# Two mixture-of-experts layers: gate and up computed transposed, each block's gate and up weights loaded into a ring of four pairs

## The reference

```python
# layer 0: E=16 experts, inner width 64, 2 experts for each token, besides a shared expert
hmid = silu(x @ w1[e].T) * (x @ w3[e].T) * combine
moe_out = hmid @ w2[e].T
# layer 1: E=32 experts, inner width 128, 4 experts for each token
gate = minimum(x @ w_gate[e] + b_gate[e], 7.0)
up = clip(x @ w_up[e] + b_up[e], -7.0, 7.0)
activated = (up + 1.0) * gate * sigmoid(1.702 * gate)
out = sum over the 4 of topk_weight * (activated @ w_down[e] + b_down[e])
```

## Time and profile before

| | us |
|---|---|
| median of 3 runs | 2014.76 (2012.57 to 2014.78) |
| the profiled execution, its own time | 2019.52 |
| its span, first to last instruction | 2017.7 |

### The profile page before, as it was taken

One profiled execution on the slowest core, in us unless ns is written; L12 is line 12 of the kernel. 1 busy time (PEld: TensorE's weight loads), 2 busy tenths in 40 slices (PEclk: granted clock), 3 DMA queues, 4 the chain that ended last, 5 costly groups with the idle time before them and its releaser, 6 DMA issues. The chain is left out here.

```text
span 2017.7 us, 47121 instructions
## 1 busy us (share of the span) xinstructions
PE 1637.8 (81%) x14340; PEld 1188.0 (59%) x14341; DVE 1447.6 (72%) x3040; ACT 950.5 (47%) x2964; POOL 1163.5 (58%) x1253
## 2 busy tenths in 40 slices
PE   4999999999999999799487429887884159999943
PEld 3777777777777777466366304444443148887822
DVE  3898998889989899666122267998996136666668
ACT  2888888878888788333133104333331023333300
POOL 1666666666666666356366404487885546666622
PEclk9999999999999999899689859998985579999965
DMA  5300000000000000212444240011115434444456
GB/s 174 118 16 16 16 16 16 16 16 16 16 18 21 16 16 8 84 65 81 143 140 126 96 148 22 12 64 58 66 56 211 166 104 146 143 150 131 124 197 220
DMA packets 100988, 164.76 MB, mean 82 GB/s; under 512 B 20031, under 2 KB 75884, under 8 KB 100336
## 3 DMA queue, kind: packets, MB, share of 16 engines
q1 hardware_dynamic: 75184, 104.37, 16.4%
q0 software_dynamic: 22272, 56.15, 7.6%
q10 hardware_dynamic: 3456, 3.34, 0.5%
HBM read 94.26 MB, written 75.76 MB: 84 GB/s over the span
## 5 line engine op out<-in xcount | busy, mean ns | idle before, releaser
L387 POOL TENSOR_TENSOR w_down<-w_down,attn_rsum 128x1024 f32<-128x1024 f32 x256 | 485.1, 1895 | 287.4 <-DVE attn_rsum L343 286.3
L303 ACT ACTIVATE w_down<-attn_ps_s,attn_negmax 128x256 f32<-128x256 f32 x1024 | 470.6, 478 | 24.9 <-DVE attn_negmax L337 21.4
L337 DVE TENSOR_REDUCE attn_negmax<-attn_ps_s 128x4 f32<-128x1024 f32 x256 | 311.9, 1218 | 28.4 <-PE attn_ps_s L225 27.5
L815 POOL DMA_INDIRECT l_by_token<-l_experts_outs,l_experts_places x240 | 236.7, 986 | 162.4 <-DVE l_experts_outs L781 88.0
L348 DVE COPY w_down<-attn_ps_t 128x1024 f32<-128x1024 f32 x256 | 312.1, 1219 | 17.5 <-PE attn_ps_t L237 14.5
L225 PE MATMUL attn_ps_s<-ctx_d,attn_q_sb 64*128 64x256 f32 x2048 | 271.6, 378 | 0.5 <-ACT w_down L303 0.5
L251 PE MATMUL attn_ps_qo<-w_down,attn_vb 128*64 128x256 f32 x2048 | 249.3, 385 | 1.3 <-DVE w_down L348 1.3
L225 PEld LDWEIGHTS attn_ps_s<-ctx_d,attn_q_sb 64*128 64x128 f32 x2048 | 219.1, 188 | 5.1 <-issue 0.8
L303 ACT ACTIVATION_READ_ACCUMULATOR w_down<-attn_ps_s,attn_negmax 128x1 f32 x1024 | 215.0, 210 | 0.0
L722 PE MATMUL l_experts_ps_gu<-w_gu,l_experts_rows_t 128*128 x960 | 210.3, 355 | 0.6 <-issue 0.2
L781 DVE TENSOR_SCALAR l_experts_outs<-l_experts_ps_y,l_experts_tails 128x256 f32<-128x256 f32 x240 | 105.1, 479 | 142.4 <-PE l_experts_ps_y L743 68.8
(11 more groups left out here) (249 smaller groups left out, 2745.2 us busy)
## 6 DMA issues: line engine op xcount, KB each, us to landing
l_experts_rows<-l_rows_in SPq DMA_DIRECT2D x240, 136.0 KB
combine_rows_got<-l_by_token SPq DMA_DIRECT2D x32, 512.0 KB, 5.5
ctx_d<-in_ctx SPq DMA_DIRECT2D x64, 128.0 KB, 2.7
combine_rows_got<-l_by_token SPq DMA_DIRECT2D x32, 256.0 KB, 3.4
w_gu<-in_w_gu SPq DMA_DIRECT2D x2, 4096.0 KB, 17.9
l_rows_in<-zeros SPq DMA_DIRECT2D x1, 4352.0 KB, 32.0
x_sb<-in_x SPq DMA_DIRECT2D x32, 128.0 KB, 2.2
w_down<-in_w_down SPq DMA_DIRECT2D x1, 4096.0 KB, 12.1
```

Of the source, the lines that this page charges most:

```text
L303: last = nc.scalar.activation(prob[:, n % 4, c, :], ps_s[:, n % 2, c, :], ACT.Exp, bias=negmax[:, n % 2, c:c + 1], accum_out=sums[:, n % 2 ...
L337: nc.vector.tensor_reduce(negmax[:, n % 2, :], ps_s[:, n % 2, :, :], AX.X, ALU.max, negate=True).then_inc(max_ready, 1)
L387: nc.gpsimd.tensor_tensor(prob[:, n % 4, :, :], prob[:, n % 4, :, :], rsum[:, n % 2, :].unsqueeze(2).to_broadcast([P, 4, A_N]), ALU.mult). ...
L815: pool.indirect_dma_start(m.by_token, bass.IndirectOffsetOnAxis(ap=places[:, r % BODY, b:b + 1], axis=0), outs[:, r % 2, b, :], None, boun ...
```

## The change

Gate and up are computed transposed: the weights are the stationary operand (`w_now`), the transposed rows are the moving one, and the result has one inner unit in each partition. So the activated block is already in the form that the down product takes, and the second transposes (L735) with their copy (L764) are gone. The bias is one number for each partition in this form: `block_tables` makes a table `block_bias` with one column for each block by two more matmuls and some DVE steps, and DVE adds the bias while it clips. The three bfloat16 terms and the bias matmul are gone.

The gate and up weights are no longer resident. SP loads for each block the weights of its expert (256 KB in layer 1, 128 KB in layer 0) from memory into `w_now`, a ring of `RING` = 4 pairs. The ring of rows grows from 4 pairs to 8 (`BODY`), that of `outs` from 2 to 4. POOL no longer copies tails: it stores with the places read straight from `rows` (an integer now), and DVE reads the weights from there too. For this reason SP, before it loads rows over those of pair r, waits until the stores of pair r have landed. POOL's `scatter` writes weight and place with two small copies instead of one (L1033).

In layer 0, where the inner width is 64, the products of the two blocks of a pair go to different halves of the array's columns, the down product uses different halves of its rows, and ACT copies each block's down weights to `down_now`.

The core of the diff:

```diff
-    BODY = 4
+    HALVES = P // I
+    BODY, RING = 8, 4
...
-        work = ph.sbuf("act_work", [P, 2, 4, 2, I])
-        outs = ph.sbuf("outs", [P, 2, 2, H])
+        w_now = ph.sbuf("w_now", [P, RING, 2, KT, 2 * I])
+        down_now = ph.sbuf("down_now", [P, RING, H]) if HALVES == 2 else None
+        gate = ph.sbuf("gate", [P, 2, 2 // HALVES, P])
...
+        outs = ph.sbuf("outs", [P, RING, 2, H])
...
+        rows_stored = [ph.sem(f"rows_stored{n}") for n in range(RING)]
...
+        w_loaded = [ph.sem(f"w_loaded{n}") for n in range(RING)]
...
             def load(it, r):
                 if not (isinstance(it, int) and it * BODY + r < BODY):
                     done(sp, x_made, it, r - BODY)
-                    done(sp, tail_ready, it, r - BODY)
+                    sp.sem_inc(passed, 1)
+                    sp.wait_ge(rows_stored[r % RING], it * (32 * BODY // RING) + 32 * ((r - BODY) // RING + 1))
                     sp.sem_inc(passed, 1)
                 _, at = nc.values_load_multi_w_load_instructions(
...
+            def load_weights(it, r):
+                e = experts_of(it, r)
+                if not (isinstance(it, int) and it * BODY + r < RING):
+                    done(sp, gu_made, it, r - RING)
+                    sp.sem_inc(passed, 1)
+                for b in range(2):
+                    sp.dma_start(w_now[:, r % RING, b, :, :].rearrange("p k n -> p (k n)"),
+                                 w_gu[:, bass.ds(e[b], 1), :, :].rearrange("p a k n -> p (a k n)")).then_inc(w_loaded[r % RING], 16)
+
             for r in range(BODY):
                 load(0, r)
+                if r < RING:
+                    load_weights(0, r)
             with sp.Fori(0, NI - 1) as it:
                 for r in range(BODY):
                     load(it, r + BODY)
+                    load_weights(it, r + RING)
+            for r in range(RING, BODY):
+                load_weights(NI - 1, r)
 
...
+            def gate_up(it, q):
+                done(pe, x_ready, it, q)
+                pe.wait_ge(w_loaded[q % RING], it * (32 * BODY // RING) + 32 * (q // RING + 1))
+                done(pe, gu_used, it, q - 2)
+                pe.sem_inc(passed, 1)
+                def product(u, b, kt):
+                    return nc.tensor.matmul(ps_gu[half(b), q % 2, u, column(b), :],
+                                            w_now[:, q % RING, b, kt, u * I:(u + 1) * I],
+                                            rows_t[:, q % 2, b, kt, :], start=(kt == 0), stop=(kt == KT - 1))
...
+                            for kt in range(KT):
+                                last = product(u, b, kt)
+                last.then_inc(gu_made, 1)
...
+            def down(it, q):
+                e = experts_of(it, q) if HALVES == 1 else None
+                done(pe, a_ready, it, q)
...
+                done(pe, y_ready, it, q - 2)
+                pe.sem_inc(passed, 1)
+                for b in range(2):
+                    weights = down_now[half(b), q % RING, :] if HALVES == 2 else \
+                        w_down[:, bass.ds(e[b], 1), :].rearrange("p a n -> p (a n)")
+                    last = nc.tensor.matmul(ps_y[:, q % 2, b, 0:H], act_t[half(b), q % RING, column(b), :], weights,
+                                            start=True, stop=True)
+                last.then_inc(y_made, 1)
...
             def step(it, r):
                 if exists(it, r + 2):
+                    transposes(it, r + 2)
                 if exists(it, r + 1):
-                                                    start=False, stop=True)
-                    last.then_inc(gu_made, 1)
-                if exists(it, r):
-                    done(pe, a_ready, it, r)
-                    done(pe, at_ready, it, r - 1)
-                    pe.sem_inc(passed, 1)
-                    for b in range(2):
-                        last = nc.tensor.transpose(ps_a[0:I, b * P:(b + 1) * P], work[:, r % 2, 3, b, :], sb["ident"][:, :])
-                    last.then_inc(at_made, 1)
+                    gate_up(it, r + 1)
                 if exists(it, r - 1):
+                    down(it, r - 1)
             run(pe, step)
...
+            def clip(n):
+                done(dve, gu_made, 0, n)
+                done(dve, a_ready, 0, n - 2)
+                for b in range(2):
+                    last = nc.vector.tensor_scalar(gate[:, n % 2, b, :], ps_gu[:, n % 2, 0, b, :],
+                                                   bias[:, 0, 2 * n + b:2 * n + b + 1], LIMIT, ALU.add, ALU.min)
+                last.then_inc(gate_ready, 1)
+                for b in range(2):
+                    last = nc.vector.tensor_scalar(up[:, n % 2, b, :], ps_gu[:, n % 2, 1, b, :],
+                                                   bias[:, 1, 2 * n + b:2 * n + b + 1], LIMIT + 1.0, ALU.add, ALU.min)
+                last.then_inc(gu_used, 1)
...
+            def product(n):
+                done(dve, function_ready, 0, n)
+                done(dve, y_made, 0, n - RING)
+                if bias is None:
...
+                    nc.vector.tensor_tensor(gate[:, n % 2, :, :], gate[:, n % 2, :, :], glu[:, n % 2, :, :], ALU.mult)\
+                        .then_inc(glu_ready, 1)
+                    dve.wait_ge(glu_ready, n + 1)
+                    nc.vector.scalar_tensor_tensor(out=act_t[:, n % RING, :, :], in0=up[:, n % 2, :, :], scalar=1.0 - LIMIT,
+                                                   in1=gate[:, n % 2, :, :], op0=ALU.max, op1=ALU.mult).then_inc(a_ready, 1)
...
+            def weigh(n):
+                done(dve, y_made, 0, n)
+                if n >= RING:
+                    dve.wait_ge(rows_stored[n % RING], 32 * (n // RING))
+                for b in range(2):
+                    last = nc.vector.tensor_scalar(outs[:, n % RING, b, :], ps_y[:, n % 2, b, 0:H],
+                                                   rows[:, n % BODY, b, WEIGHT:WEIGHT + 1], None, ALU.mult)
+                last.then_inc(y_ready, 1)
+
+            for n in range(-2, NP + 2):
+                if bias is not None and 0 <= n + 1 < NP:
+                    clip(n + 1)
+                if 0 <= n - 2 < NP:
+                    weigh(n - 2)
+                if 0 <= n < NP:
+                    product(n)
...
             def store(it, r):
                 done(pool, y_ready, it, r)
-                done(pool, tail_ready, it, r)
                 pool.sem_inc(passed, 1)
                 for b in range(2):
-                    pool.indirect_dma_start(m.by_token, bass.IndirectOffsetOnAxis(ap=places[:, r % BODY, b:b + 1], axis=0),
-                                            outs[:, r % 2, b, :], None, bounds_check=T * m.K - 1, oob_is_err=False)\
-                        .then_inc(rows_stored[r % 2], 16)
-            for r in range(2):
-                take_tails(0, r)
-            for r in range(BODY):
-                take_tails(0, r + 2)
-                store(0, r)
-            with pool.Fori(1, NI - 1) as it:
+                    place = rows[:, r % BODY, b, DEST:DEST + 1].bitcast(I32)
+                    pool.indirect_dma_start(m.by_token, bass.IndirectOffsetOnAxis(ap=place, axis=0),
+                                            outs[:, r % RING, b, :], None, bounds_check=T * m.K - 1, oob_is_err=False)\
+                        .then_inc(rows_stored[r % RING], 16)
+            with pool.Fori(0, NI) as it:
...
-        nc.gpsimd.tensor_copy(xn[:, :, H:H + 2], m.tail[:, it * 2 + q, k, :, :]).then_inc(self.tails_set, 1)
+        nc.gpsimd.tensor_copy(xn[:, :, DEST].bitcast(I32), m.place[:, it * 2 + q, k, :])
+        nc.gpsimd.tensor_copy(xn[:, :, WEIGHT], m.weight[:, it * 2 + q, k, :]).then_inc(self.tails_set, 1)
...
-            experts(nc, sb, m0, w_gu0, w_down0, None, None, Swish)
+            experts(nc, sb, m0, ins["w_gu0"], w_down0, None)
             combine0(nc, sb, m0)
-        with nc.sbuf_tensor("w_gu1", [P, m1.E, KT, 2 * m1.I], F32) as w_gu1:
-            half = m1.E // 2
-            attention1(nc, ins, sb, m1, w1, w_gu1,
-                       [(w_gu1[:, c:c + half, :, :], ins["w_gu1"][:, c:c + half, :, :]) for c in (0, half)], later_loaded)
-            wait_for(nc, later_loaded, 16 * (len(later) + 3))
-            experts(nc, sb, m1, w_gu1, w_down1, sb["bias1"], sb["term_ones"], ClippedSwish)
+        with nc.sbuf_tensor("region", [P, m1.E, KT, 2 * m1.I], F32) as region:
+            attention1(nc, ins, sb, m1, w1, region, (), later_loaded)
+        wait_for(nc, later_loaded, 16 * (len(later) + 1))
+        experts(nc, sb, m1, ins["w_gu1"], w_down1, m1.block_bias)
```

More of the change, by code:

```diff
@@ L565, in _ @@
         nc.tensor.matmul(ps[3][0:1, 256:256 + NB], blocks[:, :], below[:, :], start=True, stop=True).then_inc(pe_done, 1)
+        if tb.bias is not None:
+            pe.wait_ge(dve_done, 12)
+            for u in range(2):
+                last = nc.tensor.matmul(ps[0][0:m.I, u * 256:u * 256 + NB], tb.bias[:, u, :], tb.of_block[:, :], start=True, stop=True)
+            last.then_inc(tb.bias_made, 1)
```

(11 more changed lines are left out.)

285 lines of the change are left out of this document (109 added, 176 removed).

## The result

| | before | changed |
|---|---|---|
| median, us | 2014.77 (2012.57 to 2016.41, 4 runs) | 3007.55 (3003.18 to 3009.65, 4 runs) |
| span of the profiled execution, us | 2017.7 | 3005.9 |

The ratio is 1.492, with a 95% interval of 1.490 to 1.494. The forecast was 3038.

What follows compares the result with a forecast made beforehand. Waits for stores in SP's queue were to delay the weights, making a chain of one pair a round in layer 1: 2019.5 +937 +103 -12.4 -5.7 +2 = 3043, less 4.8 for the median, 3038 us; overall range 2800 to 3190.

Steps and rivals of the forecast that it cites:

- What bounds, and the chain: Both expert stages: SP loads weights of pair r+4 only after stores of r land; layer 1 moves one pair a round.
- The round of layer 1: Layer 1's experts: gate and up, clips, weigh, stores, landing, SP and weights sum to 15.9 us (13.3 to 17.9).
- The clock term: Layer 1's gate and up, first work after PE's pause, take 3.78 us at 1.2 GHz, against 1.99 at 2.4.
- The number of rounds: Layer 1's experts: pairs 0 to 3 load without the chain, then 76 rounds of 15.9 us make 1208.
- Layer 0: Layer 0's experts: a round of 13.4 us moves two pairs, 264 us against 161, so +103 (62 to 188).
- What is saved: Outside the two expert stages: -12.4 us in attention1, -5.7 in the setup, +2 for POOL's second copy.
- The setup: Start of the kernel: SP's first load of the next stage comes at about 22.1 instead of 27.77, -5.7 us.
- POOL behind the big load: attention1: POOL stood 13.88 us behind the 8 MB load of weights, otherwise 1.52, so -12.4 us.
- the first one: Rival for both expert stages: SP's wait for stores doesn't hold the weights back; total 1915 us, chance 0.04.
- The third, bandwidth: Rival: bandwidth bounds through 42 MB more, 226 of 295 us of all DMA engines; 1930 to 2050, chance 0.02.
- The second: Rival for layer 1: the chain moves on by two pairs a round, 8.5 us a pair; about 2475, chance 0.04.
- The signs: Profile after: layer 1 some 1240 us, L750 about 16 apart, SP waiting for `l_by_token`, layer 1's DMA share below 0.2.

Runs made afterwards that it cites:

- e1: The changed kernel with weigh(n-2) put ahead of clip(n+1) in DVE's order, SP's queue as it was; 2480.97 us.
- e2: The changed kernel with the weights of pair r+4 issued ahead of the rows of pair r+8 in SP's loop; 2387.63 us.
- e8: The changed kernel with 24 unread matmuls on PE in each pair of layer 1, ahead of the wait for weights; 2978.95 us.
- e5: The changed kernel with rows loaded 5 pairs ahead instead of 8 and weights ahead of rows in SP's loop; 2020.73 us, ratio 1.0145 to the kernel before.
- e6: e5 with weigh also put ahead of clip in DVE's order; 2034.81 us, ratio 1.010 to the kernel before.
- e10: e6 with only the first block's gate and up weights loaded for each pair and used for both blocks; 1952.25 us, ratio 0.981 to the kernel before.

## Why the prediction was right, step by step

- **What bounds, and the chain.** Right. L826 waits for L750 13.2 us in each round, SP waits for the landing of `l_by_token`, and e1 and e2 each cut one different link and got the two-pair round that follows from the same list of links.
- **The round of layer 1.** 15.9 forecast, 15.93 measured. In the round shown: gate and up to the first clip 3.80 (3.78), the clips 1.12 (0.9; their upper bound 1.15 was the right one), `weigh` 0.78 more, stores 3.14 (3.16), landing and SP until the first issue of weights 3.33 (3.37), weights 3.44 (3.7). The sum is 15.61; a round in which SP reads the next table takes about 0.4 more, as the 16.1 and 15.7 by turns show. The Trainium skill's estimate for the two weight loads, by "DMA: Bandwidth & Descriptors", section on the anatomy of one DMA, was 3.2 us; measured were 3.44 here, between it and the rows' 3.7. The section speaks of transfers that POOL issues, and these are SP's.
- **The clock term.** 3.78 against 3.75 measured at half clock, and e8 showed the other end: 2.02 at full clock, and the round shorter by 1.57.
- **The number of rounds failed.** I multiplied by 76; the chain ran 72 times. (That DVE's waits number 76, as I had written, is chance: four of them are no rounds.) SP's loop ends with the rows of pair 79, and the weights of the last four pairs are issued behind it, without a wait for stores:

```profile
2890.18 3.82 SPq L716 DMA_DIRECT2D l_experts_w_now<-in_w_gu  x4
...
2894.05 1.86 PEld L750 LDWEIGHTS l_experts_ps_gu<-l_experts_rows_t,l_experts_w_now 128*128 128x128 f32 x16
...
2897.23 1.86 PEld L750 LDWEIGHTS l_experts_ps_gu<-l_experts_rows_t,l_experts_w_now 128*128 128x128 f32 x16
```

  These follow each other every 3.2 us instead of 15.9: -51. I had written down that last loop from the diff and not counted it. With the start 19.4 us (17.5) and the end rightly sized, layer 1 cost +892 and not +937. That is 45 us, more than the 30 by which the whole forecast was too high. Layer 0 and the savings took 9 of them back. The remaining 5 came off by luck: I had taken 4.8 us off for the median, and the traced execution of the changed kernel lay at its median (3007.58 to 3007.55).
- **Layer 0.** +103 forecast, +106.6 measured, by errors that cancel, so its closeness is luck. The round took 14.1 us (DVE's products L838 at 1010.09 and 1221.24, 15 rounds apart), not 13.4: between the stores' end at 1112.05 and the first issue of weights lie 4.08, not 3.37. SP's table read comes once in two pairs, and I took half of it; but in a round over two pairs it always stands ahead of the first. That is 0.33 of the 0.71; the rest is open. And the chain held 32 pairs, not 36, for the reason above, which is 225 us of the 265.8; the start, the last four pairs and the end took the other 40, where I had put 23 for start and end.
- **What is saved.** The setup: SP's first load at 21.93 (22.1 forecast, 27.77 in the earlier trace rows). POOL behind the big load: its 23rd copy of the stage, the one behind the wait of 13.88, came 20.54 us after the 22nd, and comes 7.26 after it now,

```profile
1642.22 0.19 POOL L1033 COPY attn_xf<-l_place 128x4 int32<-128x4 int32 x1 [2.21 <-DMA l_rows_in<-attn_xf,l_routing_group_slots]
1642.35 0.19 POOL L1034 COPY attn_xf<-l_weight 128x4 f32<-128x4 f32 x1
...
1649.48 0.18 POOL L1033 COPY attn_xf<-l_place 128x4 int32<-128x4 int32 x1
```

  but only 6.1 of these 13.3 was left at the end of attention1, 10.4 forecast. POOL's second copy lies in each of the 32 turns, not in the last dozen: the turns of that stage are some 0.13 us longer throughout (the last three follow each other in 6.90 us, 6.77 before), about 4 in all, and the turn ahead of that place is 1.7 longer. That it is the copy was not tried by itself.
- **The rivals.** e5 and e6 are the first one ("the weights are there in time") and show that it was priced wrongly: I gave 1915, and e5 took 2021 and e6 2035. The third, bandwidth, gave 1930 to 2050. Both runs lie in that range, but that bandwidth is the reason is not shown. Its sum was near: I divided by the 410 GB/s of the two large loads and got 226 us of all DMA engines, and e6 shows 0.81 of 301, which is 244. A term that I had in no rival is SP's queue. I had written down 2.7 us of it for each of the first pairs; it took 3.5 in e5, more than the 3.03 that I gave PE. The second would have been e1 or e2 (2475 forecast; 2481 and 2388).
- **The signs.** The DMA share of layer 1 was to fall below 0.2, and it is 0.22. The others came as written: the stage of 1192 us, the round, SP's wait for `l_by_token`. From `weigh`'s end to the next L750 lie 9.91 us in the round shown (10.3).

## What to carry to other kernels

Where one queue carries loads for two rings, each load inherits the waits of the other. Before pricing anything, write down for each wait which pair's work it needs on every engine on the way round; the time of a pair is the round divided by the number of pairs that it moves on, and the cheapest repair is to enlarge that number (exchanging two lines took off some 600 us here). The rings' depths, 8 and 4, do not tell it; what counts is whose stores stand ahead of a load in the queue. When the chain is gone, look at the traffic next and at the issuing queue's own time for a pair, and take away one of them at a time: e10 took away both and could not tell. A resident operand that is copied on an idle engine kept the form's gain in layer 1 (0.44 us a pair).

## What I had not expected of the hardware

- The kernel before takes 1990 us on two of the chips and 2014 and 2015 on two others. The traces' spans are 1988.0 and 2017.7, and 26 of these 30 us lie in layer 0's experts, whose stores take 119.7 and 145.8 us from first to last. Layer 1, bound by PE, takes 280.2 and 282.5, and everything else agrees within 1 or 2 us. Why that stage differs is not shown; it is one in which no engine is full and the engines wait for transfers and for each other. Such kernels are compared on one chip only.
- The first matmuls after a pause run at 1.2 GHz here in nearly every round (3.75 us for gate and up); those of the last four pairs, which follow without the pause, take 1.95. Work that nobody reads, put into a pause of 10 us, brought the stage to 2.4 GHz and shortened the path.
